# Expert 3 in one wide unit as the fifth of an expert-parallel schedule, the fourth routing batch assigned beside its chunks

## Time and profile before

| | |
|---|---|
| three runs | 336.99, 337.28, 338.23 us |
| the profiled execution | 338.06 us, span 335.9 us |
| TensorE busy | 287.1 us, 85% |
| weight loads | 240.0 us, 71% |
| VectorE busy | 251.5 us, 75% |
| ScalarE busy | 217.8 us, 65% |
| GpSimd busy | 186.3 us, 55% |
| mean granted TensorE clock | 0.93 of full |

### The profile page before, as it was taken

How to read it: one execution, slowest core, us unless ns; L and a number is a source line. 1 busy time by engine, 2 the same in 40 slices (tenths; PEclk the granted TensorE clock), 3 DMA queues, 4 the chain that set the end, 5 groups by cost and what they waited for, 6 DMA issues and landing times.

```text
span 335.9 us, 5632 instructions
## 1 busy us (share of the span) xinstructions
PE 287.1 (85%) x1676; PEld 240.0 (71%) x1676; DVE 251.5 (75%) x805; ACT 217.8 (65%) x498; POOL 186.3 (55%) x154
## 2 busy tenths in 40 slices
PE   8999999968622996329999999999999999999990
PEld 5666665658611886229999987877888888889890
DVE  2799989987501894027888889989877777999985
ACT  4687987877421573026777876876765666669884
POOL 5015888788775027787864444347347337368700
PEclk9999999998985699557999999999999999999996
DMA  7996294478751005334444336264324224523664
GB/s 226 361 406 191 68 239 138 131 153 247 168 179 47 19 27 150 104 36 46 50 65 58 51 49 176 50 145 57 48 22 56 34 23 86 114 22 40 95 187 132
DMA packets 46828, 37.74 MB, mean 112 GB/s; under 512 B 7073, under 2 KB 40800, under 8 KB 46800
## 3 DMA queue, kind: packets, MB, share of 16 engines
q1 hardware_dynamic: 35392, 26.56, 26.8%
q0 software_dynamic: 11408, 10.85, 21.0%
HBM read 17.86 MB, written 17.10 MB: 104 GB/s over the span
## 4 chain that ended last, share of the span: by engine, by line
PE 71%; DVE 13%; issue 7%; another core or an unknown queue 5%; ACT 3%; ACTq 0%; POOL 0%; DVEq 0%; POOLq 0%
PE big L676 12%; PE big L674 12%; PE big L675 11%; PE big L582 5%; PE b_xnt L690 3%; PE b_xnt L693 3%; PE b_xnt L691 3%; PE b_ht L693 3%; PE b_ht L690 2%; PE b_ht L691 2%; PE b_rt L710 2%; PE b_xt L626 2%; PE big L568 1%; PE b_ht L631 1%
## 5 line engine op out<-in xcount | busy, mean ns | idle before, releaser
L878 ACT ACTIVATE act_g<-big 128x256 f32<-128x256 f32 (+1 forms) x144 | 65.4, 454 | 88.9 <-PE big L676 57.6
L674 PE MATMUL big<-x_hi,e_hi 128*128 128x256 f32 (+1 forms) x264 | 88.8, 336 | 4.1 <-issue 3.8
L675 PE MATMUL big<-x_hi,e_lo 128*128 128x256 f32 (+1 forms) x264 | 86.0, 326 | 0.0
L676 PE MATMUL big<-x_lo,e_hi 128*128 128x256 f32 (+1 forms) x264 | 86.0, 326 | 0.0
L511 POOL DMA_INDIRECT slots<-rows,slot_ix x64 | 66.3, 1035 | 35.5 <-issue 18.6
L526 POOL DMA_INDIRECT tokens<-contrib,token_ix x32 | 52.0, 1625 | 38.6 <-DVE token_ix L1169 30.6
L526 POOL DMA_INDIRECT tokens<-zero_rows,token_ix x28 | 45.6, 1629 | 32.9 <-DVE token_ix L1169 25.8
L674 PEld LDWEIGHTS big<-x_hi,e_hi 128*128 128x128 f32 x264 | 52.0, 197 | 8.0 <-issue 3.5
L676 PEld LDWEIGHTS big<-x_lo,e_hi 128*128 128x128 f32 x264 | 51.7, 196 | 4.0
L675 PEld LDWEIGHTS big<-x_hi,e_lo 128*128 128x128 f32 x264 | 52.0, 197 | 3.4
L1177 DVE TENSOR_TENSOR h<-act_g,big 128x256 f32<-128x256 f32 (+3 forms) x36 | 18.3, 509 | 18.8 <-ACT act_g L878 13.7
(11 more groups left out here) (212 smaller groups left out, 683.9 us busy)
## 6 DMA issues: line engine op xcount, KB each, us to landing
e_raw<-in_L_ffn_w_kernel_dram SPq DMA_DIRECT2D x16, 320.0 KB
slots<-zero_rows SPq DMA_DIRECT2D x8, 548.0 KB, 8.1
e_lo<-e_raw POOLq DMA_DIRECT2D x5, 544.0 KB
e_raw<-in_L_ffn_wo_kernel_dram SPq DMA_DIRECT2D x8, 320.0 KB
xd<-slots SPq DMA_DIRECT2D x16, 137.0 KB
xd<-slots SPq DMA_DIRECT2D x8, 274.0 KB
x<-in_L_attn_input_seq_dram SPq DMA_DIRECT2D x8, 256.0 KB, 4.6
tokens<-rows SPq DMA_DIRECT2D x8, 256.0 KB
```

The source lines that it names most:

```text
L674: pe.matmul(dst, e_hi[q][:, c0:c0 + m], xdt_hi[u % 2][:, 0:w], start=True, stop=False)
L675: pe.matmul(dst, e_lo[q][:, c0:c0 + m], xdt_hi[u % 2][:, 0:w], start=False, stop=False)
L676: mm = pe.matmul(dst, e_hi[q][:, c0:c0 + m], xdt_lo[u % 2][:, 0:w], start=False, stop=True)
L878: nc.scalar.activation(act0[n % RH][0:m, 0:w], pre(n, P)[0], ACT.Gelu_apprx_tanh).then_inc(gelu_ready, 1)
```

## The change

- **Units.** Expert 3 takes groups 0 to 3 in one wide unit, and this is unit 4, where it was two narrow units, 6 and 7. There are 23 units in place of 24: 0..2 as before, 3 = (0, groups 2-3), 4 = (3, groups 0-3), 5 and 6 = experts 1 and 2 on groups 2-3, then as before with every number one less. The tables keyed by units follow, and expert 3's high pieces come at (2,2), (2,5), (3,1), (3,3).
- **Fourth batch.** `places(NR - 1)` and the six assign steps move from unit 3 to unit 4.
- **Low words of expert 2.** The DMA makes the first half (pieces 0 and 1) at row tile 5 of batch 1, where it made the second half at tile 7. VectorE makes pieces 2 and 3, the second one after chunk (1,1) and not after (0,2). ScalarE's negatives are those of pieces 0 and 1, in LSTM step 6 and at (0,4), where they were two at (0,5).
- **Powers** 5 and 7 move from tiles 1 and 6 of batch 1 to tiles 2 and 5.
- **Start and end.** `w` is loaded by ScalarE's DMA queue. The outputs of groups 6 and 7 leave in halves: three from SyncE, the last half of group 6 from ScalarE.

```diff
-    NEGATIVE = {2: [(0, 0), (0, 1)], 4: [(1, 0)], 5: [(1, 1), (1, 2), (1, 3)]}
+    NEGATIVE = {2: [(0, 0), (0, 1)], 4: [(1, 0)], 5: [(1, 1), (1, 2), (1, 3)], 6: [(2, 0)]}
-    LOWS_AMONG = {(0, 3): (0, 1), (1, 2): (1, 0), (1, 3): (1, 1), (1, 7): (2, 1)}
-    ROOTS_AMONG = {(0, 3): 2, (0, 5): 3, (0, 7): 4, (1, 1): 5, (1, 3): 6, (1, 6): 7}
-    HIGH_AT = {3: [(3, 1), (3, 4), (4, 1), (4, 4)], 4: [(11, 4), (11, 5), (12, 2), (12, 3)], ...
-    LOAD_AT = {2: 4, 5: 5, 13: 6, 14: 7}
+    LOWS_AMONG = {(0, 3): (0, 1), (1, 2): (1, 0), (1, 3): (1, 1), (1, 5): (2, 0)}
+    ROOTS_AMONG = {(0, 3): 2, (0, 5): 3, (0, 7): 4, (1, 2): 5, (1, 3): 6, (1, 5): 7}
+    HIGH_AT = {3: [(2, 2), (2, 5), (3, 1), (3, 3)], 4: [(10, 4), (10, 5), (11, 2), (11, 3)], ...
+    LOAD_AT = {2: 4, 5: 5, 12: 6, 13: 7}
...
-        units = [(e, q) for part in (range(RING_E - 1), [RING_E - 1]) for q in quarters[:NB // 2] for e in part] + [(e, q) for q in quarters[NB // 2:] for e in range(2)]
+        units = [(e, quarters[0]) for e in range(RING_E - 1)] + [(0, quarters[1]), (RING_E - 1, halves[0])]
+        units += [(e, quarters[1]) for e in range(1, RING_E - 1)] + [(e, q) for q in quarters[NB // 2:] for e in range(2)]
...
-            sp.dma_start(w_raw[:, :], w_in[:, :]).then_inc(w_loaded, 16)      # SyncE
+            act.dma_start(w_raw[:, :], w_in[:, :]).then_inc(w_loaded, 16)     # ScalarE
...
-            for g in range(S):
+            for g in range(LAST):
                 sp.wait_ge(fin_ready[g], T)
                 sp.dma_start(out[g]..., fin[g][:, :, :]).then_inc(out_done, 16)
+            for h in range(2):
+                for g in range(S - 1, LAST - 1, -1):
+                    if g == S - 1 or h == 0:
+                        sp.wait_ge(fin_ready[g], T // 2 * (h + 1))
+                        sp.dma_start(half_out(g, h), half_fin(g, h)).then_inc(out_done, 16)
+            act.wait_ge(fin_ready[LAST], T)                                   # ScalarE
+            act.dma_start(half_out(LAST, 1), half_fin(LAST, 1)).then_inc(out_done, 16)
...
-                    elif (u, k) == (3, 0):
+                    elif (u, k) == (4, 0):
                         places(NR - 1)
...
-                    if (u, k) == (0, 5):
+                    if (u, k) == (0, 4):
+                        negative_weights(2, 1)
+                    elif (u, k) == (0, 5):
                         high_weights(2, 3)
-                        for n in range(PIECES // 2, PIECES):
-                            negative_weights(2, n)
...
-                    low_weights(2, 0)          # LSTM step 7
+                    low_weights(2, 2)
-            low_weights(2, 1)                  # after chunk(0, 2)
+            low_weights(2, 3)                  # after chunk(1, 1)
-            among = {(3, k): k for k in range(AS)}
+            among = {(4, k): k for k in range(AS)}
```

More of the change, by code:

```diff
@@ L54, in build @@
     NEGATIVE_FIRST = {3: [(0, 2), (0, 3)]}
-    NEGATIVE = {2: [(0, 0), (0, 1)], 4: [(1, 0)], 5: [(1, 1), (1, 2), (1, 3)]}
+    NEGATIVE = {2: [(0, 0), (0, 1)], 4: [(1, 0)], 5: [(1, 1), (1, 2), (1, 3)], 6: [(2, 0)]}
     LOW_BY_DMA = 2
-    LOWS_AMONG = {(0, 3): (0, 1), (1, 2): (1, 0), (1, 3): (1, 1), (1, 7): (2, 1)}
-    ROOTS_AMONG = {(0, 3): 2, (0, 5): 3, (0, 7): 4, (1, 1): 5, (1, 3): 6, (1, 6): 7}
-    HIGH_AT = {3: [(3, 1), (3, 4), (4, 1), (4, 4)], 4: [(11, 4), (11, 5), (12, 2), (12, 3)], 5: [(12, 4), (12, 5), (13, 2), (13, 3)],
-               6: [(13, 4), (13, 5), (14, 2), (14, 3)], 7: [(14, 4), (14, 5), (15, 2), (15, 3)]}
-    LOAD_AT = {2: 4, 5: 5, 13: 6, 14: 7}
+    LOWS_AMONG = {(0, 3): (0, 1), (1, 2): (1, 0), (1, 3): (1, 1), (1, 5): (2, 0)}
+    ROOTS_AMONG = {(0, 3): 2, (0, 5): 3, (0, 7): 4, (1, 2): 5, (1, 3): 6, (1, 5): 7}
+    HIGH_AT = {3: [(2, 2), (2, 5), (3, 1), (3, 3)], 4: [(10, 4), (10, 5), (11, 2), (11, 3)], 5: [(11, 4), (11, 5), (12, 2), (12, 3)],
+               6: [(12, 4), (12, 5), (13, 2), (13, 3)], 7: [(13, 4), (13, 5), (14, 2), (14, 3)]}
+    LOAD_AT = {2: 4, 5: 5, 12: 6, 13: 7}
     EARLY_STATS = {(-5, 1): range(0, 2), **{(-5, k): range(3 * k - 4, 3 * k - 1) for k in range(2, 6)}, (-4, 0): range(14, 16)}
@@ L324, in build, with half_out, half_fin @@
         last_bank = [b_rt, b_y[NU % 2]]
+        def half_out(g, h):
+            return out[g].rearrange("(t p) d -> p t d", p=P)[:, h * T // 2:(h + 1) * T // 2, :]
+        def half_fin(g, h):
+            return fin[g][:, h * T // 2:(h + 1) * T // 2, :]
         def unscaled(g, t):
@@ L461, in _ @@
                 load_fin(g)
-            for g in range(S):
+            for g in range(LAST):
                 sp.wait_ge(fin_ready[g], T)
                 sp.dma_start(out[g].rearrange("(t p) d -> p t d", p=P), fin[g][:, :, :]).then_inc(out_done, 16)
-            sp.wait_ge(out_done, 16 * S)
+            for h in range(2):
[3 more added lines that the diff above has]
+                        sp.dma_start(half_out(g, h), half_fin(g, h)).then_inc(out_done, 16)
+            sp.wait_ge(out_done, 16 * (S + GB))
         @block.gpsimd
```

## The result

The changed kernel took 345.33 us (median of four, 341.61 to 345.90), the kernel before beside it 337.75: ratio 1.022, 95% interval 1.017 to 1.027. It is slower by 7.6 us; I had forecast 2.5 faster. The profiled execution took 345.90 us, its span 343.7.

What follows compares the result with a forecast made beforehand. TensorE was taken to bound 150.2 to 320 us, with stalls beside GpSimd's scatter runs before. Terms -2.9 + 0.5 - 0.1 + 0.6 + 0 - 0.6 + 0 = -2.5: 335.6 profiled, 334.8 median; range 331.2 to 339.4.

Steps and rivals of the forecast that it cites:

- Part 1: Expert 2's low DMA and powers 5 and 7 moved in batch 1: -2.9 us, bounds +3 and -6.3.
- the lead: Unit 2 starting at about 84, not 88.9: 5 us, of which 1.5 chunks, 1.6 us, were taken as gain.
- rival C: Slower: 22 unbroken scatters, stall from 83 in unit 1, 5.0 us lost; +2.7 in all, 340.0; chance 0.15.
- Part 4: Fourth batch's scatters start after the wide unit, at 131, and the stall catches units 5 and 6: 0, bounds -3 and +3.
- part 3: One wide unit for two narrow ones: -0.1; a second pair of narrow-wide borders: +0.6, bounds 0 and 1.3.
- The border: The second pair of borders, narrow to wide and back, around the new wide unit: +0.6 us, bounds 0 and 1.3.
- Part 2: Expert 3's high and low words wanted two units sooner, TensorE waiting in unit 3's end: +0.5 us, 0 to 1.1.
- The end: Last outputs in halves from two queues: -0.6 us, 0 to -1.0; by the skill's rule alone -0.4.
- The start: w loaded on ScalarE's queue, SyncE's list one issue earlier: 0, bounds -0.1 and +0.4 us.
- A: The lead at unit 2 survives whole: -6.3 us in place of -2.9, 331.4; chance 0.14.
- B: First long stall ends where it did, the low-DMA move gives 0: sum +0.4, 337.7; chance 0.22.
- D: Low DMA at tile 5 waits for ScalarE's late negatives, run ends 1.3 us later: 339.0; chance 0.07.

Runs made afterwards that it cites:

- e2: The kernel before with only expert 2's low DMA at tile 5, powers 5 and 7 moved, and its low-word and negative pieces moved; 345.10 us, ratio 1.012.
- e16: The edit of e2 on the kernel before, run a second time on another chip; 341.85 us, ratio 1.016.
- e3: The changed kernel with the fourth batch assigned in narrow unit 3, as in the kernel before; 341.11 us, ratio 0.999 to the kernel before.
- e13: The changed kernel with the edits of e1 and e3 together, leaving the wide unit, expert 3's earlier words, start and end; 331.84 us, ratio 0.985.
- e1: The changed kernel with expert 2's low DMA and powers 5 and 7 back at their old tiles; 342.83 us, ratio 1.004 to the kernel before.
- e6: The kernel before with only the fourth batch's scatters paced by waits for gelus, three chunks a tile; 323.00 us, ratio 0.947.
- e5: The kernel before with third and fourth batches' scatters paced by waits for gelus, three and two and a half chunks a tile; 315.58 us, ratio 0.927.
- e11: The kernel before with both batches' scatters paced evenly, one row tile per 2.75 chunks, on a chip without late signals; 302.84 us, ratio 1.001.
- e4: The kernel before with a small GpSimd multiply ahead of every second row tile of the third and fourth batches; 340.95 us, ratio 0.998.
- e7: The kernel before with the fourth batch's scatters sending 8 of 137 words per row to a small separate tensor; 339.21 us, one run.
- e15: e11 with the change's start and end added, on a chip with late signals; 309.19 us, ratio 0.921 to the kernel before.
- e9: The changed kernel with third and fourth batches' scatters paced by the gelus, on a chip without late signals; 304.92 us, ratio 1.009.
- e10: e9 with the bank pairs of the wide units from unit 11 on swapped; 303.52 us, ratio 1.003 to the kernel before.
- e17: e10 run again, also on a chip without late signals; 303.52 us, ratio 1.002 to the kernel before.

## Why the prediction was wrong

**Part 1 is the step that failed**: forecast -2.9 us, measured +4 to +6 (e2, e16, e3 against e13, the change against e1). Its details came nearly as worked out: the wait at power 5 went (power 6 waited 1.64 us in its place), unit 2's wait of 2.87 us went, the run ended at 105.8 (105.4 forecast), the stall began at about 83. What failed is the price of that last point. I had written that "the stall will bite sooner, near 83", and still took 1.5 chunks of gain from the lead. The gelus from chunk 4 of unit 1 on came 5.7, 8.5 and 9.9 us apart, not 5.6 to 7.7, and most of the lead was gone before unit 2 began: 87.6, not 84. That the first stall begins in unit 1 and holds it was among my own signs of being wrong. This is rival C in its place and mechanism (22 scatters, begin in unit 1, chunk 3 of unit 2 not through when the run ends), to which I gave 0.15; it still put part 1 at only +2.3 in all (5.0 lost, 2.7 given back), about half of what the runs say, and its total of 340.0 was too low for that and for part 4. "Against: the stall seen before 80 should go with the shorter run there" held, in part: units 0 and 1 gained 1.7 us of work. It was too little.

**Part 4** is the second: forecast 0 with bounds of 3 us either way, measured +6.5 (e1 against e13) against the same kernel with the batch in unit 3. The scatters started at 140.3, not at 131. My step "as many chunks are lost in it, as both are narrow" compared units 5 and 6 with unit 5 of the kernel before. The right comparison was with what would have stood beside the scatters had they not been moved: the wide unit. That may also be why **part 3**, forecast at +0.5 with its borders, was worth -5 us with the start and the end (e13). The two errors leave +1.5 between them. Here, too, the comparison is shown and its reason argued.

**The border** of part 3 was forecast 0.6 late at the new pair; the 1.3 us came at the old one, through the order of the banks, which I had left out.

**Part 2** was right: forecast +0.5, and the wide unit's first matmul starts 0.2 us after expert 3's last low words, having waited 0.70 (VectorE's and TensorE's timelines):

```profile
125.14 0.71 DVE L1097 TENSOR_TENSOR e_lo<-e_raw,e_hi 128x544 fp32r<-128x544 f32 x1
```

```profile
126.06 0.48 PE L687 MATMUL big<-x_hi,e_hi 128*128 128x512 f32 x1 [0.70 <-issue]
```

**The end** gave 0.8 (forecast 0.6): the three halves and the last one left as said, 2.7 us from the last row to the span's end, 3.6 before:

```profile
339.47 1.50 ACT L925 ACTIVATE x<-b_rt,root_b,root_y 128x128 f32<-128x128 f32 x4 [1.27 <-DVE root_b L1341]
341.01 0.48 ACTq L938 DMA_DIRECT2D out_dram<-x  x1
```

On the rule of the Trainium skill that the prediction weighed (page "DMA: Bandwidth & Descriptors", section "Issuing engines are not separate DMA queues") this decides nothing. ScalarE's transfers stand in the changed kernel's list of queues under a number of their own (q10, 416 packets), and the gain was 0.2 above what the forecast gave, 0.4 above what I took from the rule; but the halves make the last transfer smaller, too, and weren't tried apart from the queue.

**The start** was neutral. The 0.6 us lost before unit 0 need not be the change's: they stand at a wait of VectorE for "remote" of 1.06 us at 53.19, ahead of what part 1 moves, and unit 0's turn stands at 64.0 in e6 and 64.7 in e5, which have the old start. As to the rivals: A and B fell with the longer stall, D did not happen (the low DMA followed the power without a wait). The chance of "slower" was added up wrongly: C, half of D and a tenth of the rest are 0.26, not 0.19.

## What to carry to other kernels

When a stall is seen beside a piece of work on another engine, price every move by what will stand beside that work afterwards, and test the coincidence first: one wait in a loop (as in e6 or e5) would have shown in a single run that spacing is worth 18 to 25 us, where my forecast for moving a transfer was 2.9. A long burst of GpSimd's indirect DMAs that nobody needs at once can be paced by the progress of the consumer; here it cost nothing measurable where there was nothing to cure (e11, 0.999 to 1.003). And when one chip gives a wait whose releaser no view can name, measure on a second chip before tuning against it, and count how many of its signals the trace has recorded.

## What the runs showed of the hardware

- TensorE's signals come late beside back-to-back indirect scatters (one per 1.3 us) on some chips and not on others: gelus wait up to 12 us for matmuls that the trace shows as done. In the kernel before, TensorE's signals stand in the trace at 100.72 and 108.45, just ahead of the gelus of 100.81 and 108.54, though the last matmuls recorded before them end at 97.3 and 103.3. A 0.2 us instruction every four scatters doesn't help (e4), smaller rows don't (e7, one run), rests of 0.5 to 6 us do (e5, e6, e15). Beside wide chunks the last gelu in time stood 12 us into the run of scatters in e13, but 6 in e3. Adds, one per 1.9 us, run from 154 us on in the kernel before with no late gelu beside them.
- The chips differ in a second thing. In all 14 profiles from chips with late signals 13 to 23 of the 138 or 144 signals of gelus left no record (17 in the kernel before, 13 in the changed one, 22 each in e5 and e15, which have next to no late waits); in all 6 profiles from chips without, every one has a record. Late signals and lost records come from the same chips; this is a coincidence in 20 profiles, not yet a cause.
- All of this looks like something that fills when scatters and matmuls together come too fast, and drains in rests. What it is stays open, and the plainest rival was not tested: the recording itself. The Trainium skill, page "NOTIFIC — the notification-queue block", section "7.1 Overflow: three behaviours, one of which stalls the engine", says that the block that writes the trace records holds its producers back when its internal queues are full, and loses none there; records can be lost where the ring in memory is full. Every run here was recorded, so none can show which of it happened, and if recording holds TensorE up, the 34 to 38 us belong to the measurement and not to the kernel.
- Also open: whether the change by itself, without pacing, costs anything on a chip without late signals, and whether its paced form keeps pace with e15 on one that has them (e9, e10 and e17 all fell on chips without).
